# Causal latent attention and an eight-expert layer: projection and routing issued as single matmuls between the scores, own code for the first projection and the last routing, W1 loaded stack by stack

## The chip, the core and the metric

One core of a Trainium2 chip runs the whole program. The metric is the device time of one execution in microseconds (us); lower is better. The engines are PE (TensorE), DVE (VectorE), ACT (ScalarE), POOL (GpSimd) and SP (SyncE, which here only issues DMAs and waits). Each has its own in-order instruction stream; semaphores order them against each other.

## The reference

Four sequences of 1024 tokens, 256 channels, fp32. An attention block with 16 heads of 16 channels and a latent of 64 for keys and values, then a mixture of experts that sends each token to the two best of eight experts:

```python
xn   = layernorm(x)                                # x: (4, 1024, 256)
c_kv = xn @ W_DKV                                  # (.., 64)
k, v = c_kv @ W_UK, c_kv @ W_UV                    # 16 heads of 16
q    = xn @ W_UQ
ctx  = softmax(causal(q k^T / 4)) @ v
x    = x + ctx @ W_O
xf   = layernorm(x)
topw, topi = top_k(xf @ Wr / temp, 2); topw = softmax(topw)
for e in range(8):
    a, g = split(xf @ W1[e] + b1[e], 2)
    out += (a * silu(g) @ W2[e] + b2[e]) * weight_of(e)
x    = x + out
```

## The kernel before

**Two phases.** `fused_phase` does the attention, the output projection, the router, and scatters each token's normalised row into the lists of its two experts in DRAM (`slot_rows`). `expert_phase` then runs over 71 tiles of 128 rows of these lists. The change touches only the first phase.

**The step loop.** Every engine's stream in the fused phase is one Python loop over steps `s`. The work is cut into 16 quads (four heads of one sequence) of 12 units; a unit is one step. In step `s` PE computes the four score blocks whose row maxima DVE takes (`max_scores`, line 1009, line 1020 in the trace; DVE lines 745 and 748; three PSUM banks between them), the four score blocks of a unit `LEAD` = 16 steps earlier, with the maxima folded in as two extra rows (`prob_scores`, line 1039; ACT takes the exponential, line 961; three banks), and the product with V of a unit 18 steps earlier (`products`, line 1060, into one bank). POOL masks the diagonal blocks (`causal`, line 600). After the maxima of a quad are complete, PE turns them (line 1071), ACT copies them to SBUF (line 952), and SP writes them into the stack of Q by four DMAs (line 425). `TOTAL` is 192 steps; a sequence is a `PERIOD` of 48.

**Projection.** A chunk is 512 tokens, two to a sequence. SP loads x, DVE takes the statistics (`chunk_norm`), POOL the inverse root and the normalised rows (`normalise`, line 572), and PE then has nine steps, one group each (`project`, line 1074): two of four transposes (line 1081), the latent (line 1086), two for q (line 1093), two for k (line 1097), two for v (line 1101). A group is issued as a block at the end of the step, after `products`, into the one bank `x_aux_ps`; ACT copies it out at the start of the next step. POOL splits q and k into two float parts (`split`, lines 580 and 582), SP stores them, and later loads the stacks of a quad from there (`load_stack`, line 404). The loop starts at step -48, so the two chunks of the first sequence go through the same code with no scores beside them; chunks 2 to 7 run beside the scores from steps 6 and 17 of each period.

**Routing.** For each sequence: the softmax denominators are inverted and spread by DMA (lines 457 and 462), POOL scales the heads (line 610), four PE groups apply W_O (line 1111), ACT copies, POOL adds the residual (line 618), DVE takes statistics, POOL normalises (line 624), four PE groups transpose (line 1121), PE computes the logits (line 1131), DVE chooses the experts and the slots, POOL scatters 16 times (line 646). Sequences 0 to 2 are routed beside the scores of the next; for the last, the same code runs after the scores, one group after the other through `x_aux_ps`.

**Weights.** W1 lies where the stacks were and W2 where the probabilities were. ACT issues all 16 loads (12 MB) after the last product (`load_weights`, line 964).

## Time and profile before

| | us |
|---|---|
| median of 3 runs | 1404.23 |
| lowest and highest run | 1403.85, 1408.58 |
| the profiled execution | 1409.86 |
| its span | 1408.1 |
| PE busy | 1162.7 (83%) |
| DVE busy | 694.8 (49%) |
| ACT busy | 497.5 (35%) |
| POOL busy | 476.7 (34%) |

The profile is one execution. Times in its rows are us from the start of its span, means of one instruction are ns. "PEclk" is TensorE's granted clock as a share of full speed: 1.00 is 2.4 GHz, 0.50 is 1.2 GHz, and a value between is a stretch with both. A row of a timeline has start, duration, engine, line, instruction, tiles and count, and in brackets how long the engine was idle before it and what ended that. "PEld" is the loading of the stationary operand. A row of a window has the stretch and its length, the busy time and the number of instructions of PE, PEld, DVE, ACT and POOL, PEclk, the mean busy share of the 16 DMA engines, and GB/s moved. A busy PE is not a PE at its peak: matmuls are pipelined, and the durations overlap.

### The profile page before, as it was taken

To read this page: it belongs to the slowest core of one execution; us is meant where nothing else is said; L and a number is where in the kernel's file an instruction comes from. 1 tells how busy PE (TensorE), PEld (TensorE's weight loads), DVE (VectorE), ACT (ScalarE), POOL (GpSimd) and SP (SyncE) were. 2 spreads that over 40 slices of the span, in tenths; PEclk is the share of its full clock that TensorE was granted. 3 is DMA by queue.
4 is the path that set the end of the run, shared out by engine and by line. 5 is a ranking of instruction groups with operands and counts; after the bars stand their busy time and mean duration, and the time that the engine had idled before them with its cause. 6 is when DMAs were issued, how large, how long until landed. Compare 5 with 4: busy or idle time off the path is not lost. (4 is left out here: it accounts for less than half of the span.)

```text
span 1408.1 us, 19071 instructions
## 1 busy us (share of the span) xinstructions
PE 1162.7 (83%) x5236; PEld 612.5 (43%) x5237; DVE 694.8 (49%) x2121; ACT 497.5 (35%) x1077; POOL 476.7 (34%) x547
## 2 busy tenths in 40 slices
PE   3577999898989798989998870332999999999995
PEld 1234444344444334534445320221666666666663
DVE  1065587555665455576665400130555555555553
ACT  1102576554645454555554540010222222222221
POOL 6324313424425633424145330442222222222222
PEclk9655999879857697775588655555999999999998
DMA  2576343365404454322510129415222222222222
GB/s 81 173 129 174 100 96 70 113 177 138 100 8 136 143 165 111 69 57 83 153 55 17 40 76 346 112 61 194 39 46 47 46 45 45 45 45 45 45 45 34
DMA packets 94890, 130.39 MB, mean 93 GB/s; under 512 B 26208, under 2 KB 71136, under 8 KB 94816
## 3 DMA queue, kind: packets, MB, share of 16 engines
q1 hardware_dynamic: 64608, 89.51, 23.7%
q0 software_dynamic: 13296, 17.77, 7.7%
q10 hardware_dynamic: 16912, 22.23, 5.4%
q8 instruction: 34, 0.56, 0.2%
q14 instruction: 40, 0.33, 0.1%
HBM read 74.60 MB, written 54.22 MB: 91 GB/s over the span
## 5 line engine op out<-in xcount | busy, mean ns | idle before, releaser
L961 ACT ACTIVATE m_prob<-b_prob_ps 128x512 f32<-128x512 f32 (+3 forms) x768 | 326.2, 496 | 191.1 <-PE b_prob_ps L1039 185.8
L745 DVE CUSTOM_DVE_ANT_0 b_max_ps<-b_max_ps,b_mask_max 128x256 f32<-128x256 f32 (+3 forms) x512 | 245.9, 503 | 265.8 <-PE b_max_ps L1020 265.1
L1020 PE MATMUL b_max_ps<-m_stacks 48*128 48x512 f32 (+3 forms) x768 | 301.9, 501 | 54.9 <-DVE b_neg_max L745 29.5
L1039 PE MATMUL b_prob_ps<-m_stacks 50*128 50x512 f32 (+3 forms) x768 | 293.9, 483 | 27.6 <-DMA m_stacks<-b_max_rows 15.1
L1020 PEld LDWEIGHTS b_max_ps<-m_stacks 48*128 48x128 f32 x768 | 160.6, 237 | 234.1 <-DVE b_neg_max L745 111.3
L1268 POOL DMA_INDIRECT out_dram<-e_y,e_token x71 | 111.1, 1565 | 323.2 <-DVE e_y L1320 311.9
L1060 PE MATMUL b_acc_ps<-m_prob,b_v_aug 128*32 128x512 f32 (+3 forms) x1536 | 218.5, 651 | 0.2 <-POOL m_prob L600 0.2
L748 DVE TENSOR_REDUCE b_neg_max<-b_max_ps 128x1 f32<-128x512 f32 x256 | 176.1, 688 | 58.6 <-PE b_max_ps L1020 57.8
L600 POOL TENSOR_SCALAR_AFFINE_SELECT m_prob<-m_prob 128x512 f32<-128x512 f32 x128 | 80.6, 638 | 335.4 <-ACT m_prob L961 335.0
L1039 PEld LDWEIGHTS b_prob_ps<-m_stacks 50*128 50x128 f32 x768 | 150.7, 235 | 69.6 <-ACT m_prob L961 34.4
L1387 PE MATMUL e_g_ps<-m_w,e_rowsT 128*128 x284 | 135.5, 600 | 0.5 <-DVE e_rowsT L1288 0.5
L1404 PE MATMUL e_y_ps<-m_w,e_hiddenT 128*128 x568 | 134.4, 379 | 1.8 <-ACT e_hiddenT L1350 1.8
L1387 PE MATMUL e_a_ps<-m_w,e_rowsT 128*128 x284 | 133.9, 594 | 0.0
L1404 PEld LDWEIGHTS e_y_ps<-m_w,e_hiddenT 128*128 128x128 f32 x568 | 107.8, 190 | 46.2 <-issue 35.2
L1345 ACT ACTIVATE e_gate<-e_g_sum 128x512 f32<-128x512 f32 x71 | 44.7, 629 | 166.4 <-DVE e_g_sum L1300 166.4
L1350 ACT ACTIVATE e_hiddenT<-e_hiddenT_ps 128x512 f32<-128x512 f32 x71 | 42.4, 597 | 168.3 <-PE e_hiddenT_ps L1395 168.3
L1300 DVE TENSOR_TENSOR e_g_sum<-e_g_ps,e_b 128x512 f32<-128x512 f32 x71 | 49.1, 692 | 83.8 <-PE e_g_ps L1387 83.8
L1111 PE MATMUL x_aux_ps<-c_wo,c_heads 128*128 128x256 f32 x128 | 40.1, 467 | 55.7 <-POOL c_heads L610 53.6
L1387 PEld LDWEIGHTS e_a_ps<-m_w,e_rowsT 128*128 128x128 f32 x284 | 54.3, 191 | 68.8 <-issue 68.8
L1303 DVE TENSOR_TENSOR e_hidden<-e_a_ps,e_b 128x512 f32<-128x512 f32 x71 | 49.1, 691 | 71.0 <-PE e_a_ps L1387 71.0
L745 DVE DVE_READ_ACCUMULATOR2_ANT b_neg_max<- 128x1 f32 x512 | 72.3, 141 | 0.0
L1387 PEld LDWEIGHTS e_g_ps<-m_w,e_rowsT 128*128 128x128 f32 x284 | 48.9, 192 | 35.4 <-issue 35.4
(148 smaller groups left out, 1049.2 us busy)
## 6 DMA issues: line engine op xcount, KB each, us to landing
e_rows<-slot_rows ACTq DMA_DIRECT2D x73, 129.0 KB, 2.1
q_parts<-a_part SPq DMA_DIRECT2D x16, 512.0 KB, 2.7
k_parts<-a_part SPq DMA_DIRECT2D x16, 512.0 KB, 3.0
m_stacks<-q_parts SPq DMA_DIRECT2D x32, 256.0 KB, 5.2
m_stacks<-k_parts SPq DMA_DIRECT2D x32, 256.0 KB, 7.2
ctx_cols<-b_ctx_out SPq DMA_DIRECT2D x16, 512.0 KB
m_w<-in_L_ffn_W ACTq DMA_DIRECT2D x8, 1024.0 KB, 17.7
a_x<-in_L_attn_x SPq DMA_DIRECT2D x8, 512.0 KB, 4.1
```

The source lines that it names most:

```text
L600: nc.gpsimd.affine_select(out=tile, in_=tile, compare_op=ALU.is_ge, fill=0.0, base=0, pattern=[[0, QUAD], [1, P]], channel_multiplier=-1). ...
L745: nc.vector.tensor_tensor_reduce(scores, scores, mask_max[:, HALF - width:HALF], -1.0, -MASKED, ALU.add, ALU.min, to).then_inc(max_done, 1)
L748: nc.vector.tensor_reduce(to, scores, AX.X, ALU.max, negate=True).then_inc(max_done, 1)
L961: nc.scalar.activation(prob[:, n % NP, 0:width], prob_ps[n % NS][:, 0:width], ACT.Exp, scale=SCALE).then_inc(prob_ok, 1)
L1020: nc.tensor.matmul(out_ps[:, 0:width], q_st[g % RING][at:at + STACK, j, i * P:(i + 1) * P], k_st[g % RING][at:at + STACK, j, half * HALF:h ...
L1039: nc.tensor.matmul(prob_ps[n % NS][:, 0:width], k_st[g % RING][at:at + MAXROWS, pair, j * P:(j + 1) * P], q_st[g % RING][at:at + MAXROWS, ...
L1060: mm = nc.tensor.matmul(acc_ps[32 * h:32 * h + 2 * HD, first:first + width], v_aug[g % 2][:, j, h, :, :].rearrange("p r s -> p (r s)"), pr ...
L1268: nc.gpsimd.indirect_dma_start(out=out, out_offset=bass.IndirectOffsetOnAxis(ap=token[c % B][:], axis=0), in_=y[c % B][:], in_offset=None, ...
L1300: nc.vector.tensor_tensor(g_sum[c % 2][:], g_ps[c % 2][:], bias_of(expert, 0, FF, FF), ALU.add).then_inc(g_sum_ok, 1)
L1303: nc.vector.tensor_tensor(hidden[c % 2][:], a_ps[c % 2][:], bias_of(expert, 0, 0, FF), ALU.add).then_inc(a_sum_ok, 1)
L1387: last = nc.tensor.matmul(out_ps[:], rowsT[c % 2][:, d * P:(d + 1) * P], w1_sb[:, bass.ds(expert, 1), d, first:first + FF].rearrange("p e ...
L1404: last = nc.tensor.matmul(y_ps[c % 2][:], hiddenT[c % 2][:, f * P:(f + 1) * P], w2_sb[:, bass.ds(expert, 1), f, :].rearrange("p e n -> p ( ...
```

## The change

- **Projection beside the scores.** A chunk has 12 steps instead of nine: the latent and each q group are cut into their two matmul calls, one to a step. The PE work of a step (`aux`) comes after the second of the four score pairs, not at the end; ACT's copy comes after the third exponential of the same step. W_O is cut in the same way (8 steps instead of 4). The chunks start at steps 7 and 19.
- **DVE normalises** the chunk and the routed rows; POOL did both.
- **First projection.** Chunks 0 and 1 have code of their own ahead of the loop, which now starts at step 0. It uses all eight PSUM banks. ACT copies the high part straight from PSUM, DVE subtracts. Before the first score PE and DVE wait for the small weights, as before (`small_in`); SP now issues those behind the first stack, the last parts, V and the load of V.
- **Last routing.** The last sequence has code of its own behind the loop: heads scaled and residual added by DVE, four banks, transposed rows copied by ACT and DVE in turn.
- **Weights.** SP loads two experts' W1 whenever one of the last four stacks is no longer read; the last two and all of W2 are issued behind the last sequence's spread.
- **Order of SP's work.** A stack is loaded 12 steps ahead of its quad, was 18; x2 is loaded after the spread; some later steps of the routing are one to six steps later.

```diff
-CHUNK_AT = [6, 17]
-CHUNK_STEPS = 9
+CHUNK_AT = [7, 19]
+CHUNK_STEPS = 12
+GROUP_OF = [0, 1, 2, 2, 3, 3, 4, 4, 5, 6, 7, 8]
+SPLIT_AT = [6, 8, 9, 10]
-SPREAD_AT, ADD_AT, NORMAL_AT = 26, 28, 37
-ROUTER_AT, COUNT_AT, SCATTER_AT = 42, 46, 50
+HEADS_AT, ADD_AT, NORMAL_AT = 27, 32, 44
+ROUTER_AT, COUNT_AT, SCATTER_AT = 48, 52, 55
...
@@ sync @@
+            for n in range(4):
+                store_start_part(n)
+            load_stack(0)
+            for n in range(4, 8):
+                store_start_part(n)
+            for n in range(4):
+                store_start_v(n)
+            load_x(2)
+            load_v(0)
+            sp.dma_start(wo[:], w_o.rearrange("(c p) n -> p c n", p=P)).then_inc(small_in, 16)
+            sp.dma_start(wr[:], w_r.rearrange("(c p) n -> p c n", p=P)).then_inc(small_in, 16)
+            sp.dma_start(temp_in[:], temp.rearrange("(o n) -> o n", o=1).to_broadcast([P, 1])).then_inc(small_in, 16)
+            for s in range(LAST):
...
+                if u == 0 and NQUAD - RING <= g < NQUAD - 1:
+                    free_stack(g)
...
+            load_x2(LATE)
+            load_heads(LATE)
+            spread_den(LATE)
+            free_stack(NQUAD - 1)
+            sp.wait_ge(pv_ok, TOTAL)
+            for e in range(EXPERTS):
+                sp.dma_start(w2_sb[:, e, :, :], w2[e].rearrange("(f p) n -> p f n", p=P)).then_inc(w_in[e], 16)
...
@@ vector @@
+            def normalise(chunk, t):
+                if t == 0:
+                    dve.wait_ge(rstd_ok, chunk - 1)
+                    if chunk > 2:
+                        dve.wait_ge(aux_ps_ok, aux_at["project", chunk - 1, TURN_GROUPS - 1] + 1)
+                nc.vector.tensor_scalar(xn[:, t, :], x_in[:, t, :], mean_var[:, t, 0:1], rstd[:, t:t + 1],
+                                        ALU.subtract, ALU.mult).then_inc(xn_ok, 1)
...
+            def start_rest(n):
+                dve.wait_ge(start_hi_ok, n + 1)
+                nc.vector.tensor_tensor(start_part[n][:, 1, :].bitcast(F32R), start_ps[(6 + n) % 8][:],
+                                        start_part[n][:, 0, :], ALU.subtract).then_inc(start_lo_ok, 1)
...
+            invert(LATE)
+            for k in range(2 * DC):
+                late_heads(k)
+            for t in range(PAIRS):
+                late_residual(t)
+                late_statistics(t)
+            batch_norm(LATE)
+            for t in range(BT):
+                normalise2(LATE, t)
...
@@ scalar @@
+                for q in range(QUAD):
+                    if 0 <= s - LEAD < TOTAL:
+                        exponential((s - LEAD) * QUAD + q)
+                    if q == 2:
+                        aux_copies(s)
...
@@ tensor @@
+            start_turn(0)
+            start_turn(1)
+            pe.wait_ge(w_project_in, 32)
+            start_latent(0)
+            start_latent(1)
...
+            for n in range(4):
+                start_values(n)
+            pe.wait_ge(start_lo_ok, 8)
+            pe.wait_ge(start_v_ok, 4)
+            pe.wait_ge(const_ok, ROUTE_CONSTS)
+            pe.wait_ge(small_in, 48)
+            for s in range(LAST):
...
+                for q in range(QUAD):
+                    n = s * QUAD + q
+                    if s < TOTAL:
+                        max_scores(n)
+                    if 0 <= s - LEAD < TOTAL:
+                        prob_scores(n - LEAD * QUAD)
+                    if q == 1:
+                        aux(s)
+                if 0 <= s - LEAD - LAG < TOTAL:
+                    products(s - LEAD - LAG)
+            for t in range(PAIRS):
+                late_add(t)
+            for t in range(PAIRS):
+                late_normal(t)
```

## Rows read from the trace of the kernel before

**Rows 1.** Windows: the four stages of the run.

```profile
0.00:74.49 74.49, 31.93 (x65) 12.53 (x66) 4.36 (x22) 12.04 (x20) 35.80 (x62) 0.80 0.44 128
74.49:838.24 763.75, 690.50 (x3526) 321.97 (x3526) 442.94 (x1535) 389.62 (x902) 289.39 (x371) 0.74 0.38 99
838.24:974.65 136.41, 23.13 (x82) 17.84 (x83) 17.82 (x66) 8.76 (x13) 40.41 (x44) 0.53 0.54 166
974.65:1408.00 433.35, 417.17 (x1564) 260.14 (x1564) 229.72 (x498) 87.08 (x142) 111.08 (x71) 0.98 0.29 52
```

**Rows 2.** Timeline of the first stage, rows of POOL, PE and SP.

```profile
11.22 4.85 POOL L572 TENSOR_SCALAR a_xn<-a_x,a_mv,a_rstd 128x256 f32<-128x256 f32 x4
...
19.79 3.67 PE L1086 MATMUL x_aux_ps<-a_xnT,a_wdkv 128*64 128x512 f32 x4 [0.69 <-ACT a_xnT L900]
...
24.14 1.98 PE L1093 MATMUL x_aux_ps<-a_xnT,a_wuq_rh 128*128 128x512 f32 x4 [0.68 <-ACT a_ckvT L902]
...
29.49 1.12 PE L1097 MATMUL x_aux_ps<-a_ckvT,a_wuk_rh 64*128 64x512 f32 x2 [0.69 <-ACT a_raw L909]
...
62.97 1.73 SPq L404 DMA_DIRECT2D m_stacks<-q_parts  x4
...
74.49 0.87 PE L1020 MATMUL b_max_ps<-m_stacks 48*128 48x256 f32 x3 [13.13 <-DMA m_stacks<-k_parts]
```

**Rows 3.** Windows: the end of the first stage, with the DMA rate.

```profile
35.00:70.00 35.00, 18.86 (x39) 7.54 (x37) 0.00 (x0) 6.56 (x11) 14.26 (x15) 0.65 0.56 175
```

**Rows 4.** Waits of SP: us in total, times, longest us.

```profile
SPq L437 <- DMA ctx_cols<-b_ctx_out: 23.1, 4, 9.0
...
SPq L462 <- DMA inv_dens<-c_inv_den: 15.6, 4, 12.0
```

**Rows 5.** Timeline of the last routing, all engines.

```profile
867.92 1.33 SPq L462 DMA_DIRECT2D c_spread<-inv_dens  x2
...
889.18 4.92 POOL L610 TENSOR_TENSOR c_heads<-c_heads,c_spread 128x512 f32<-128x512 f32 x4 [49.30 <-DMA c_spread<-inv_dens]
...
891.81 3.75 PE L1111 MATMUL x_aux_ps<-c_wo,c_heads 128*128 128x256 f32 x8 [53.63 <-POOL c_heads L610]
...
908.99 0.25 POOL L554 TENSOR_SCALAR c_var_eps<-c_mv 128x8 f32<-128x8 f32 x1 [1.62 <-DVE c_mv L782]
...
912.25 9.67 POOL L624 TENSOR_SCALAR c_first_row<-c_x,c_mv,c_rstd 128x256 f32<-128x256 f32 x8
```

**Rows 6.** Timeline of SP: the spread of the first sequence.

```profile
318.01 1.37 SPq L462 DMA_DIRECT2D c_spread<-inv_dens  x2
```

**Rows 7.** Timeline of POOL: the first user of that spread.

```profile
328.52 1.28 POOL L610 TENSOR_TENSOR c_heads<-c_heads,c_spread 128x512 f32<-128x512 f32 x1 [3.13 <-DMA c_spread<-inv_dens]
```

**Rows 8.** Timeline of ACT: copies of the turned maxima, twelve steps apart.

```profile
167.11 0.27 ACT L952 ACTIVATE b_max_rows<-b_max_ps 64x128 f32<-64x128 f32 x1 [1.59 <-PE b_max_ps L1071]
...
197.85 0.27 ACT L952 ACTIVATE b_max_rows<-b_max_ps 64x128 f32<-64x128 f32 x1 [0.53 <-PE b_max_ps L1071]
...
658.46 0.27 ACT L952 ACTIVATE b_max_rows<-b_max_ps 64x128 f32<-64x128 f32 x1 [1.78 <-PE b_max_ps L1071]
...
701.51 0.27 ACT L952 ACTIVATE b_max_rows<-b_max_ps 64x128 f32<-64x128 f32 x1 [1.78 <-PE b_max_ps L1071]
```

**Rows 9.** Windows: two stretches of the score stage at 1.2 GHz.

```profile
269.00:300.00 31.00, 29.84 (x124) 13.87 (x117) 12.57 (x36) 12.16 (x32) 14.09 (x17) 0.50 0.61 158
631.00:716.00 85.00, 84.16 (x370) 36.62 (x368) 48.27 (x156) 41.11 (x95) 26.35 (x33) 0.50 0.39 105
```

**Rows 10.** Timeline of ACT where it waits for POOL.

```profile
267.33 0.60 ACT L909 ACTIVATE a_raw<-x_aux_ps 128x512 f32<-128x512 f32 x1 [3.14 <-POOL a_part L582]
```

**Rows 11.** Windows of tile x_aux_ps on PE: length, PE busy (instructions), clock, DMA.

```profile
143.00:838.00 695.00, 121.50 (x397) 0.76 0.35 94
```

**Rows 12.** Timeline of a step at 2.4 GHz, one row of PE.

```profile
201.86 0.50 PE L1020 MATMUL b_max_ps<-m_stacks 48*128 48x512 f32 x1 [0.50 <-DVE b_neg_max L745]
```

**Rows 13.** The instructions of line 1320: duration ns min/median/max.

```profile
L1320 DVE TENSOR_SCALAR e_y<-e_y,e_rows x71: 352/353/451, 994.2 to 1396.4; 128x256 f32<-128x256 f32 x71
```

More of the change, by code:

```diff
@@ L244, in fused_phase @@
         second_row = sb("c_second_row", [P, BT, ROW])
+        start_x, start_xn, start_xnT, start_ckvT = x2, first_row, heads, spread[0:LAT, 0, :]
+        start_part = [prob[:, START_PARTS + 2 * n:START_PARTS + 2 * n + 2, :] for n in range(6)] + [
+            part[n][:].bitcast(F32) for n in range(2)]
         tokens = [P, BT, EXPERTS]
```

657 lines of the change are left out of this document (429 added, 228 removed).

## Prediction, made before the changed kernel ran

> **What bounds the kernel now.** I read the windows by stage first, then a timeline of each stage, then the waits. Four stages follow each other with almost no overlap [rows 1]: projection of the first sequence, 74.5 us; the scores, 763.8 us; the last routing, 136.4 us; the experts, 433.4 us. The last isn't touched, so the sum is made over the first three. In the first and the third PE is busy 32 and 23 us: these are chains, not loads. In the second PE is busy nine tenths of the time at a mean clock of 0.74. As the clock has only the levels 2.4 and 1.2 GHz (1.00 and 0.50), that is about 48% of the stage, 367 us, at the upper one and 397 us at the lower.
>
> What the lower level costs is seen where little else than scores runs: twelve steps take 197.85 - 167.11 = 30.7 us early on and 701.51 - 658.46 = 43.1 us late [rows 8], the latter inside a stretch at 0.50 throughout [rows 9]. So a us at 2.4 GHz becomes 1.40 at 1.2, and one at 1.2 gives back 0.29.
>
> **First stage.** Chunk 0's chain starts as before. From the normalised rows on (11.2 us), two chunks now go through it: eight rows of 0.35 on DVE, taken from a DVE instruction of the same shape [rows 13], against 4.85 for four on POOL [rows 2]; some 4.4 of transposes; two latents of 3.67; four q groups of 1.98; four k groups of 1.12 [rows 2]. 11.2 + 2.8 + 4.4 + 7.3 + 7.9 + 4.5 = 38.1, plus one copy after the transposes and one after the latent, 39. The first stack needs only the first four parts, which are out some 6 us earlier, at 33 to 34, and landed by 38. Before, stack loads issued from 62.97 gave the first score at 74.49, 11.5 us later [rows 2]. By that alone the scores would start at 49.5.
>
> Something else is late then. PE and DVE wait for the three small loads (`small_in`) before the first score, and SP now issues them last: behind the stack (1.5 MB), four parts (2 MB), V (1 MB) and the wait for V to land. 4.5 MB from 38 on at the 175 GB/s of the last such stretch [rows 3] end at 64; at one and a half times that rate (the stretch had its DMA busy 0.56 of the time) at 55. Then come the issue and the landing of the small loads, some 4 us, estimated from the like steps. I take 60, between 50 (if they come in time) and 68. **Gain 14, from 6 to 24.** Behind PE's wait stands the whole score stage, behind DVE's the maxima.
>
> **Last routing.** From the last copy of the context to the scaled heads it takes 50 us now. Three pieces of that lie beside 12 MB of weights on ACT's queue. The store of the context was waited for 9.0 us, the other three times (23.1 - 9.0)/3 = 4.7; the inverse denominators 12.0 against (15.6 - 12.0)/3 = 1.2 [rows 4]; the spread took 889.18 - 867.92 = 21.3 [rows 5] against 328.52 - 318.01 = 10.5 for the first sequence [rows 6, 7], itself beside other stores. The change puts six experts' W1 before the end and the rest behind the spread. Gain 4.3 + 10.8 + 10.8 = 26; less (13) if the x2 load ahead or the weights right behind still crowd these transfers, up to 31 if the spread beats its row. Moved W1 loads, three times 2 MB on SP's queue, stand ahead of the stores and of `load_max_rows` of the last quads; twelve steps last 30 us or more, 2 MB some 8, so I cost them at nothing; with that cover gone, 1 to 2 us of PE each.
>
> The Trainium skill (DMA: Bandwidth & Descriptors, the paragraph "Arbitration") says that a DMA engine takes turns between the queues that have work, packet by packet. By that rule two queues halve the spread's rate and one queue in order doesn't, which is the 21.3 against 10.5 above; the sum would stay.
>
> From the first scaled head to the router: heads by DVE, 1.2 earlier; the four W_O groups in four banks without copies between, 17.2 us between 891.81 and 908.99 [rows 5], of which 4 x 3.75 at half clock can't go, gain 2; the eight normalised rows 2.8 instead of 9.67 [rows 5, 13], gain 6.9. **Together 26 + 10 = 36, from 23 to 44.** What follows (logits, choice, sixteen scatters, the first rows of the experts) is the same work. W2 is in long before its first use: 6 MB behind the spread is some 20 us, and more than 60 us of chain follow.
>
> **Scores.** Projection and routing hold PE 121.5 us between 143 and 838 [rows 11], with the sixth chunk, before that stretch, some 136. The matmuls are the same ones. At the end of a step they are paid in full: DVE and ACT run dry behind them. Between two score pairs they can hide in what PE waits for anyway: in a clean step at 2.4 GHz PE stands 0.50 us for a bank that DVE holds [rows 12], and one matmul call is 1.98/2 = 0.99. So half of it hides, and only at the upper clock; at 1.2 GHz PE had no such gap (84.2 of 85 us busy, [rows 9]). The mean of 0.76 there [rows 11] is 0.52 of the time at the upper level: 136 x 0.52 x 0.5 = 35. Bounds: 0 and 70.
>
> DVE gains 24 normalised rows of the chunks and 24 of the routes, 48 x 0.353 = 17 us [rows 13]. At 2.4 GHz it is nearly as loaded as PE, so 0.52 of that is paid: -9 (0 to -17). The rows go off POOL, and with them a collision: at 267.3 ACT had waited 3.14 us for POOL's split [rows 10], exponentials stood behind that copy and PE behind them, and then the clock was low for 31 us [rows 9]. This falls once in each later pair of chunks, twice. 2 x (3.1 + 31 x 0.29) = 24; I take 20, since the clock may fall for another reason a little later. **Sum 35 - 9 + 20 = 46, from -17 to 94.** Stacks loaded 12 steps ahead instead of 18 cost nothing: 11.5 us [rows 2] against 30.7; were that cover gone, each of 15 quads would wait.
>
> **Total.** 14 + 36 + 46 = 96. The profiled execution took 1409.9 (span 1408.1), so 1314; it lies 5.7 above the median of the three runs. Median 1404.2 - 96 = **1308**.
>
> **Rivals.**
> - *The clock stays up.* One matmul in nearly every step, and fewer stalls, hold the upper level through most of the scores. All 397 us at 1.2 GHz would give back 397 x 0.29 = 115; half to three quarters of that, less the 20 already counted, is 37 to 66: 1308 becomes some 1255. The Trainium skill (TensorE: Matmul & The Clock Gate, "Part 1: The HAM clock gate") has activity release the clock and idleness lower it, which speaks for this. Against it stands a row: from 631 to 716 PE was busy 84.2 of 85 us and the clock remained 0.50 [rows 9].
> - *The scores give nothing.* Inserted between pairs, the calls cost what they cost at the end, and DVE's new work is paid. Only the ends gain: 1404 - 50 = 1354, between 1340 and 1375. For it: half the stage has a saturated PE.
> - *Slower.* Spread thin, projection and routing no longer lift the clock. The stretch at 0.50 ended at 716 beside such work, and what was dense is now one call to a step. If all 367 us at 2.4 GHz went to 1.2: 367 x 0.40 = 147, and 1404 - 50 + 147 = 1501. It decides from 50/0.40 = 125 us of lost upper clock on. Against it: early in the stage pure scores held 1.00 for a whole quad (30.7 us for twelve steps).
> - *The change doesn't do what it says*: the small loads hold the start at 74, and another transfer holds the spread; with scores unchanged, about 1400.
>
> **How the numbers follow.** Forecast 0.50 (1280 to 1335), clock up 0.20, scores give nothing 0.23, slower 0.05, no effect 0.02. The range leaves out the lower third of the clock case (0.07), the upper part of the third (0.05) and the last two (0.07): 1245 to 1362. About 0.5%, 7 us, is what a measurement here can tell from no change. Faster 0.93, same 0.02, slower 0.05.
>
> **What would show it.** The first score near 60, with PE's wait ended by a small load or DMA, not by the stack. From the last context copy to the first scaled head 20 to 28 us, not 50; the logits some 36 us sooner after that copy than now. In the score stage a mean clock of 0.70 to 0.85 and twelve clean steps still near 31 us at 1.00; ACT no longer waiting for `split`. DVE's normalising rows near 0.35. I am wrong if the score stage is not shorter by 20 to 80 us, above all if its clock has left that band, or if a transfer at either end waits on something that I put at nothing.

## The result, and the profile after

| | before | after |
|---|---|---|
| median of four runs, us | 1406.4 | 1377.9 |
| lowest and highest | 1403.85, 1427.19 | 1361.48, 1398.81 |
| the profiled execution | 1409.86 | 1362.01 |

The changed kernel is faster: ratio 0.9688, 95% interval 0.9645 to 0.9732, some 44 us (0.0312 x 1404.2). The forecast was 96. Executions of one and the same kernel differ here in the clock that TensorE was granted, so the ratio goes by the undisturbed ones (after: 1361.48 and 1362.01 us at a mean clock of 0.795 and 0.796; it leaves out 1393.85 and 1398.81 at 0.771 and 0.764), while the medians below are those of all executions and a few numbers are given at equal clock.

The windows by stage of the changed kernel, with the columns of [rows 1]:

```profile
0.00:60.06 60.06, 23.03 (x65) 11.71 (x66) 16.28 (x41) 10.24 (x17) 11.49 (x38) 0.87 0.56 165
60.06:824.43 764.37, 686.03 (x3526) 300.29 (x3526) 476.96 (x1584) 393.41 (x902) 226.54 (x318) 0.72 0.40 106
824.43:926.76 102.33, 20.14 (x82) 17.83 (x83) 27.12 (x84) 5.17 (x7) 25.53 (x33) 0.55 0.56 167
926.76:1359.90 433.14, 417.38 (x1564) 260.72 (x1564) 229.80 (x498) 87.07 (x142) 110.67 (x71) 0.98 0.29 52
```

Against [rows 1]: the first stage 60.06 us instead of 74.49 (14.4 less), the scores 764.37 instead of 763.75 (nothing), the last routing 102.3 instead of 136.4 (34.1 less), the experts alike. Start and last routing came as forecast; all that is missing is missing from the scores.

**Start.** Timeline, the first score, and SP's issues of the stack and of the small loads:

```profile
36.59 1.73 SPq L465 DMA_DIRECT2D m_stacks<-q_parts  x4
...
54.84 0.36 SPq L478 DMA_DIRECT2D b_v_in<-v_rows  x1
55.24 0.58 SPq L562 DMA_DIRECT2D c_wo<-in_L_attn_W_O  x1
55.87 0.47 SPq L563 DMA_DIRECT2D c_wr<-in_L_ffn_Wr  x1
56.38 0.47 SPq L564 DMA_DIRECT2D c_temp<-in_L_ffn_temp  x1
...
60.06 0.87 PE L1243 MATMUL b_max_ps<-m_stacks 48*128 48x256 f32 x3 [19.50 <-DMA c_temp<-in_L_ffn_temp]
```

PE stood 19.5 us, and what ended it was a scalar, `c_temp`, not the stack issued at 36.59. SP reached the small loads only at 55.24, behind V.

**Last routing.** Timeline of all engines, the rows that answer to [rows 5]:

```profile
824.43 0.60 ACT L1133 ACTIVATE b_ctx_out<-b_acc_ps 128x512 f32<-128x512 f32 x1 [2.89 <-PE b_acc_ps L1283]
...
838.80 0.33 SPq L515 DMA_DIRECT2D inv_dens<-c_inv_den  x1
840.72 1.33 SPq L520 DMA_DIRECT2D c_spread<-inv_dens  x2
...
854.14 2.50 DVE L907 TENSOR_TENSOR c_heads<-c_heads,c_spread 128x512 f32<-128x512 f32 x4 [15.37 <-DMA c_spread<-inv_dens]
...
875.47 6.97 PE L1353 MATMUL x_aux_ps<-c_wr,c_heads 128*128 128x8 f32 x32 [0.83 <-issue]
```

The first scaled head comes 29.7 us after the context copy (854.14 - 824.43), before 50.9. The spread took 13.4 us, before 21.3 [rows 5].

**Scores.** PE was idle for 78.3 us of the stage (764.37 - 686.03), before 73.3 [rows 1], though the waits that the prediction spoke of are smaller. The list of PE's waits (total, times, longest) names a new one at its head:

```profile
PE b_prob_ps L1262 <- DMA m_stacks<-b_max_rows: 44.3, 6, 18.5
...
PE b_max_ps L1243 <- DVE b_neg_max L827: 22.9, 35, 4.1
```

These are the rows of maxima, 8 KB a load, that SP writes into the stack (`load_max_rows`) one step before the first probability scores of a quad read them. Before, this wait was 15.1 us, 4.6 at most. Of the 44.3 us, 39.4 fall into three holes, one in each sequence that is routed beside scores. Timeline around the first of them, SP and PE and POOL:

```profile
289.42 1.37 SPq L520 DMA_DIRECT2D c_spread<-inv_dens  x2
290.75 0.27 ACT L1141 ACTIVATE b_max_rows<-b_max_ps 64x128 f32<-64x128 f32 x1 [0.46 <-PE b_max_ps L1294]
290.83 0.46 SPq L527 DMA_DIRECT2D c_x<-in_L_attn_x  x1
292.56 2.12 SPq L441 DMA_DIRECT2D q_parts<-a_part  x1
294.72 3.46 SPq L488 DMA_DIRECT2D m_stacks<-b_max_rows  x4
...
302.27 1.26 POOL L696 TENSOR_TENSOR c_heads<-c_heads,c_spread 128x512 f32<-128x512 f32 x1 [3.52 <-DMA c_spread<-inv_dens]
...
306.04 0.61 POOL L666 CAST a_part<-a_raw 128x512 fp32r<-128x512 f32 x1 [1.93 <-DMA q_parts<-a_part]
...
306.82 0.79 PE L1262 MATMUL b_prob_ps<-m_stacks 50*128 50x512 f32 x1 [9.92 <-DMA m_stacks<-b_max_rows]
...
509.19 0.79 PE L1262 MATMUL b_prob_ps<-m_stacks 50*128 50x512 f32 x1 [10.95 <-DMA m_stacks<-b_max_rows]
...
688.89 0.79 PE L1262 MATMUL b_prob_ps<-m_stacks 50*128 50x512 f32 x1 [18.50 <-DMA m_stacks<-b_max_rows]
```

ACT has the rows at 291.0. SP issues them at 294.72, behind the spread (1 MB), x2 (1 MB, which the change moved from the load of the heads to here) and a part (0.5 MB). They land when these 2.5 MB are through: the spread is used at 302.27, the room that the part's store frees at 306.04, the rows at 306.82. The stack (1.5 MB), issued three steps ahead of the rows instead of nine, stands in front as well. The Trainium skill (DMA: Bandwidth & Descriptors, "Arbitration") has the engines take turns between queues; within one queue these rows show none of that, 8 KB waited for 2.5 MB.

The longest hole has a second piece. SP and ACT around the third:

```profile
657.48 2.72 SPq L465 DMA_DIRECT2D m_stacks<-k_parts  x4
...
662.71 0.34 SPq L515 DMA_DIRECT2D inv_dens<-c_inv_den  x1
664.85 0.27 ACT L1141 ACTIVATE b_max_rows<-b_max_ps 64x128 f32<-64x128 f32 x1 [0.53 <-PE b_max_ps L1294]
672.21 1.33 SPq L520 DMA_DIRECT2D c_spread<-inv_dens  x2
...
674.10 4.94 SPq L488 DMA_DIRECT2D m_stacks<-b_max_rows  x4
```

Here ACT had the rows at 665.1, but SP issued them only at 674.10: it stood up to 9.1 us until the store of the inverse denominators, issued right behind the stack, had landed. From SP's list of waits (total, times, longest):

```profile
SPq L520 <- DMA inv_dens<-c_inv_den: 13.9, 4, 9.1
```

So two small transfers wait in that queue, and the second holds SP itself.

### The profile page after: what moved, and what is told of

It is laid out like the page before. It is cut to its first block and busy times, and to the rows that moved or that the text cites. A ratio compares the mean times of both kernels' runs of the same rounds, so it can differ in the third digit from the quotient of the medians.

```text
span 1359.9 us, 19012 instructions
## 1 busy us (share of the span) xinstructions
PE 1146.6 (84%) x5236; PEld 590.6 (43%) x5237; DVE 750.2 (55%) x2206; ACT 495.9 (36%) x1068; POOL 374.2 (28%) x459
## 5 line engine op out<-in xcount | busy, mean ns | idle before, releaser
L1149 ACT ACTIVATE m_prob<-b_prob_ps 128x512 f32<-128x512 f32 (+3 forms) x768 | 340.8, 495 | 306.4 <-PE b_prob_ps L1262 300.7
L1262 PE MATMUL b_prob_ps<-m_stacks 50*128 50x512 f32 (+3 forms) x768 | 305.8, 493 | 49.3 <-DMA m_stacks<-b_max_rows 44.3
L1243 PE MATMUL b_max_ps<-m_stacks 48*128 48x512 f32 (+3 forms) x768 | 300.7, 493 | 45.5 <-DVE b_neg_max L827 22.9
L1243 PEld LDWEIGHTS b_max_ps<-m_stacks 48*128 48x128 f32 x768 | 151.8, 234 | 264.3 <-DVE b_neg_max L827 126.4
L1283 PE MATMUL b_acc_ps<-m_prob,b_v_aug 128*32 128x512 f32 (+3 forms) x1536 | 209.7, 628 | 1.3 <-POOL m_prob L686 1.3
L1713 PEld LDWEIGHTS e_y_ps<-m_w,e_hiddenT 128*128 128x128 f32 x568 | 108.0, 190 | 46.0 <-issue 35.2
L1683 PE MATMUL e_rowsT_ps<-e_ident,e_rows 128*128 128x128 f32 x144 | 28.1, 278 | 41.3 <-DMA e_rows<-slot_rows 41.3
```

The lines of the kernel that those rows point to most:

```text
L1149: nc.scalar.activation(prob[:, n % NP, 0:width], prob_ps[n % NS][:, 0:width], ACT.Exp, scale=SCALE).then_inc(prob_ok, 1)
L1243: nc.tensor.matmul(out_ps[:, 0:width], q_st[g % RING][at:at + STACK, j, i * P:(i + 1) * P], k_st[g % RING][at:at + STACK, j, half * HALF:h ...
L1262: nc.tensor.matmul(prob_ps[n % NS][:, 0:width], k_st[g % RING][at:at + MAXROWS, pair, j * P:(j + 1) * P], q_st[g % RING][at:at + MAXROWS, ...
L1283: mm = nc.tensor.matmul(acc_ps[32 * h:32 * h + 2 * HD, first:first + width], v_aug[g % 2][:, j, h, :, :].rearrange("p r s -> p (r s)"), pr ...
L1713: last = nc.tensor.matmul(y_ps[c % 2][:], hiddenT[c % 2][:, f * P:(f + 1) * P], w2_sb[:, bass.ds(expert, 1), f, :].rearrange("p e n -> p ( ...
```

## The experiments

The ratios are to the kernel before, timed beside each version; none is on record for e1 and e5. Since the clock differs between executions, the last columns put every run at a mean clock of 0.80 with the slope that the runs of one kernel show among themselves (130 runs, 10.0 us for each 0.01 of clock). In e13 one execution at a clock of 0.607 (1617 us) is left out of these columns. That column is a way to read the runs and no cause: what a kernel does may set its clock too.

| run | what | median us | ratio (interval) | clock | at 0.80 |
|---|---|---|---|---|---|
| | before | 1411.8 | | 0.797 | 1412 |
| | after | 1377.9 | 0.969 (0.965-0.973) | 0.782 | 1361 |
| e1 | x2 as before | 1375.7 | | 0.783 | 1352 |
| e2 | spread behind rows | 1336.2 | 0.940 (0.927-0.954) | 0.803 | 1337 |
| e3 | stack earlier | 1368.7 | 0.966 (0.955-0.978) | 0.789 | 1356 |
| e4 | e2 and e3 | 1327.3 | 0.939 (0.930-0.948) | 0.810 | 1337 |
| e5 | two queues | 1358.7 | | 0.792 | 1349 |
| e6 | e4, end of step | 1365.8 | 0.971 (0.963-0.979) | 0.798 | 1365 |
| e7 | e4, POOL normalises | 1336.8 | 0.952 (0.944-0.960) | 0.801 | 1338 |
| e8 | e4, small loads early | 1325.7 | 0.941 (0.932-0.950) | 0.801 | 1327 |
| e10 | e4, late weights | 1345.0 | 0.943 (0.933-0.953) | 0.807 | 1350 |
| e11 | e8 and x, x2 early | 1307.3 | 0.917 (0.907-0.926) | 0.810 | 1319 |
| e13 | e4, dense | 1323.3 | 0.938 (0.926-0.950) | 0.820 | 1339 |
| e14 | e6, dense | 1363.0 | 0.965 (0.958-0.972) | 0.796 | 1359 |
| e17 | e11, dense | 1342.0 | 0.953 (0.945-0.962) | 0.787 | 1330 |
| e12 | before, rows first | 1391.9 | 0.984 (0.981-0.988) | 0.811 | 1403 |
| e9 | before, inserted | 1445.9 | 1.020 (1.011-1.030) | 0.778 | 1420 |
| e15 | e9, rows first | 1441.4 | 1.026 (1.015-1.036) | 0.771 | 1411 |
| e16 | e15, DVE normalises | 1413.6 | 1.003 (0.996-1.009) | 0.788 | 1401 |

### Is it the one queue? (e1 to e5)

The theory: the rows of maxima wait in SP's queue behind large transfers. Rivals: SP only issues them late; what PE no longer waits for them it waits for DVE. The first edit is e1, the second e2, the third e3; e4 is the second and the third.

```diff
 if at_route(s, HEADS_AT - 6):
     load_heads(at_route(s, HEADS_AT - 6)[0])
+    load_x2(at_route(s, HEADS_AT - 6)[0])
 if at_route(s, HEADS_AT - 2):
     spread_den(at_route(s, HEADS_AT - 2)[0])
-    load_x2(at_route(s, HEADS_AT - 2)[0])
```

> The changed kernel with one load put back: x2 (1 MB) goes with the load of the heads, four steps ahead of the spread, as before the change, and no longer right behind the spread. Theory (one queue in order): PE's 44.3 us of waiting for the rows of maxima come from tiny transfers (8 KB) that stand in SP's queue behind the spread, x2, a part and the stack. In the changed trace 2.5 MB issued from 289.42 were through at 306, so 1 MB is some 6.6 us; three sequences, so the waits for the rows fall from 44 to some 27 us and the ratio to the kernel before from 0.969 to 0.957. Rival (the issue is late, not the transfer): SP is held by its own waits, and x2 out of the way changes nothing, 0.969. Rival (the backlog only moves): x2 with the heads pushes the stack back by the same 1 MB, and the waits keep over 38 us, 0.965 to 0.969.

Measured: the waits for the rows fell from 44.3 to 28.5 us (longest 9.7), as expected to 2 us. So bytes in front of them are what they wait for, and the backlog doesn't simply move. The median stayed at 1375.7, at the changed kernel's mean clock (0.783 and 0.782); at 0.80, where every execution is put at the same clock, it is 9 us faster, of an expected 17.

```diff
 for s in range(LAST):
+    if turned_at(s - 1) is not None:
+        load_max_rows(turned_at(s - 1))
...
-                if at_route(s, HEADS_AT - 2):
-                    spread_den(at_route(s, HEADS_AT - 2)[0])
-                    load_x2(at_route(s, HEADS_AT - 2)[0])
+                if at_route(s, HEADS_AT - 5):
+                    store_inverse(at_route(s, HEADS_AT - 5)[0])
+                if at_route(s, HEADS_AT - 3):
+                    spread_den(at_route(s, HEADS_AT - 3)[0])
+                    load_x2(at_route(s, HEADS_AT - 3)[0])
```

`HEADS_AT` is 30 here, so the inverse denominators are stored in step 25 of the sequence as before and the spread goes in step 27. `store_inverse` is the first half of `spread_den`.

> The changed kernel with the rows of maxima first in each step of SP, and the spread and x2 behind them (three steps later than now, POOL's scaling three steps later too); the stacks as in the changed kernel. Theory (one queue in order): only the tail of the stack stands ahead of the rows, so the three long waits (9.9, 11.0 and 18.5 us) fall to 3 us or less each, the sum from 44 to some 12: ratio 0.946 by that alone. The clock fell at 300, 502 and 672, in these waits, and stayed low for 41, 34 and 34 us; if they caused that, up to 109 x 0.29 = 31 us more come back, 0.924. Rival (the clock falls for another reason): it falls a little later all the same, the mean clock of the score stage stays 0.72, 0.946. Rival (insertion costs what the end of the step cost): what PE no longer waits for the rows it waits for DVE, under 15 us come back, 0.96.

Measured: no wait for the rows is left in the list, and 1336.2 us, 0.940. PE now waits 18.8 us, four times, for POOL's masking (`b_acc_ps <- POOL m_prob`; 1.3 us in the changed kernel). The expected 0.946 was for the rows alone, 0.924 with the clock; the mean clock of the score stage was 0.72, that of the changed kernel. The rival on the clock holds: the falls at 300, 502 and 672 were not what kept it low. The rival on DVE is out, its wait is 25.3 us against 22.9. The rival that SP only issues the rows late isn't told apart here, since they now go ahead of SP's wait as well; e1 is against it for the first two holes (9.9 and 11.0 us became 5.2 and 8.6, with the rows still issued behind the spread), e3 for the third.

```diff
-g, u = divmod(s + UNITS, UNITS)
-if u == 0 and 0 < g < NQUAD:
+g = stack_at(s)
+if g is not None:
     load_stack(g)
```

> The changed kernel with the stacks loaded 18 steps ahead as before the change (the first of a sequence 9 ahead, behind the rows of maxima, since its parts are not stored sooner), not 12 ahead, which is three steps in front of the rows. The prediction put this move at nothing. Theory (one queue in order): 1.5 MB leave the queue ahead of the rows; the wait at 248.86 (3.3 us) goes and the three long ones lose some 2 to 5 us each, together 8 to 15: ratio 0.958 to 0.963. Rival (the move costs nothing, as predicted): spread and x2 alone make the waits, under 3 us, 0.967 to 0.970.

> Both moves of SP's work together: rows of maxima first, spread and x2 behind them, stacks 18 steps ahead. Theory (one queue in order): nothing large is left ahead of the rows, their waits fall from 44 to under 6 us: ratio 0.942 from that alone, 0.92 if the upper clock comes back as well (mean of the score stage 0.78 and more). Rival (the clock falls for another reason): 0.942, mean clock 0.72. Rival (insertion hides nothing): waits for DVE take the place of those for the rows, 0.955 or more.

e3: waits for the rows 35.2 instead of 44.3 us, 0.966; 9 us of waiting as expected, but the time can't be told from the changed kernel's (at equal clock 5 us less). Eight of the nine are in the third hole, 10.5 instead of 18.5 us: with the stack out of the way SP's longest wait for the inverse denominators is 1.2 us, not 9.1. Putting that move at nothing was wrong, by about what a measurement shows. e4: no wait for the rows, 0.939, hardly more than e2. The windows of its score stage:

```profile
60.66:796.18 735.52, 678.19 (x3526) 292.34 (x3526) 474.52 (x1584) 393.72 (x902) 226.56 (x318) 0.73 0.43 110
```

28.8 us shorter than in the changed kernel, of which 21 are idle time (57.3 against 78.3). Not all 44 us came back: in e4 POOL waits 9.5 us, until 506.91, for a part's store that now stands behind spread and x2, causal masks stand behind POOL, and PE waits 8.55 us for them. It is the same in the first sequence, so the first two holes only changed their owner: 9.9 and 11.0 us behind the rows became 9.0 and 8.6 behind POOL's masks. Most of the idle time that came back is the third hole, 18.5 us, where 4.0 are left (for scaled heads). The queue is as full as ever; the order only picks who waits. PE in e4:

```profile
313.71 1.51 PE L1297 MATMUL b_acc_ps<-m_prob,b_v_aug 128*32 128x384 f32 x8 [9.00 <-POOL m_prob L700]
...
509.51 1.51 PE L1297 MATMUL b_acc_ps<-m_prob,b_v_aug 128*32 128x384 f32 x8 [8.55 <-POOL m_prob L700]
...
679.54 2.04 PE L1346 MATMUL x_aux_ps<-c_wo,c_heads 128*128 128x256 f32 x4 [3.96 <-POOL c_heads L710]
```

For e5 these loads go to ACT's stream:

```diff
+                if at_route(s, HEADS_AT - 1):
+                    spread_den(at_route(s, HEADS_AT - 1)[0])
+                    load_x2(at_route(s, HEADS_AT - 1)[0])
                 if at_route(s, COUNT_AT):
                     power_of(at_route(s, COUNT_AT)[0])
```

> The changed kernel, in which ACT issues the spread and x2 of the first three sequences on its own queue, one step later than SP does now; SP's order is otherwise that of the changed kernel (rows of maxima behind a part and the stack). Theory (the rows wait in SP's queue behind the large transfers): in a queue of their own the large transfers no longer stand ahead of them, though the bytes are the same and move at the same time; PE's waits for the rows fall from 44 to under 15 us, ratio to the kernel before 0.945 to 0.95. Rival (the DMA engines as a whole are busy, whichever queue): the waits stay over 30 us, 0.96 to 0.97.

Measured: waits for the rows 15.0 us, so the queue matters and not only the DMA engines as a whole. In the first two sequences spread and x2 were still issued before the rows (302.43 and 304.65 us, 503.24 and 503.90), one step later than in the changed kernel, and PE waited 6.9 and 3.5 us instead of 9.9 and 11.0; in the third the rows went first (668.19, the spread 674.51), and no wait is left. The time is 1358.7, less gain than expected, with a wait that I had not foreseen. ACT must wait for the inverse denominators to land before it may issue the spread, and in the third sequence, behind the stack again, they were slow:

```profile
665.75 0.34 SPq L515 DMA_DIRECT2D inv_dens<-c_inv_den  x1
...
674.51 1.22 ACTq L1170 DMA_DIRECT2D c_spread<-inv_dens  x2
675.83 0.41 ACTq L1177 DMA_DIRECT2D c_x<-in_L_attn_x  x1
676.34 1.22 ACT L1152 ACTIVATE m_prob<-b_prob_ps 128x256 f32<-128x256 f32 x4 [8.18 <-issue]
```

ACT's exponentials stood 8.2 us behind that wait and PE 7.15 behind them. The queue that is free of large transfers belongs to an engine on the path.

### What the place of the matmuls is worth (e6, e13, e14)

```diff
-        if q == 1:
-            aux(s)
     if 0 <= s - LEAD - LAG < TOTAL:
         products(s - LEAD - LAG)
+    aux(s)
```

> The version with both moves of SP's work (0.939), and in it the matmuls of projection and routing at the end of each step behind the products, as before the change, with ACT's copies at the start of the next step; one call to a step as in the changed kernel. Theory of the prediction (between two score pairs half of each call hides at 2.4 GHz): 136 us x 0.46 of the time at the upper level x 0.5 = 31 us are paid again, ratio 0.961, and DVE waits for PE behind the calls. Rival (insertion hides nothing, PE is saturated): 0.939 within 0.006. Rival (it is the spreading over more steps that hides them, not the place in the step): 0.939 to 0.945.

Measured: 1365.8 against 1327.3, 38 us (28 at equal clock); expected 31. The size fits, the mechanism only in part: PE waits 74 times for a bank that DVE holds instead of 35 times (37.0 and 23.4 us), but of the 30 us by which the profiled score stage is longer only 7 are idle time of PE (64.3 against 57.3); the other 23 are in its busy time, and why isn't shown. Two windows of score stages, e6 and then e13 (between the pairs, whole groups):

```profile
60.28:825.96 765.68, 701.37 (x3526) 322.44 (x3526) 467.67 (x1584) 388.93 (x903) 226.52 (x318) 0.73 0.41 106
```

```profile
60.95:775.29 714.34, 652.09 (x3526) 288.68 (x3526) 476.10 (x1584) 392.40 (x902) 227.84 (x318) 0.77 0.44 113
```

e13 and e14 differ from e4 and e6 by the groups of a chunk's projection (W_O stays cut), and its splits come two to three steps sooner:

```diff
-CHUNK_STEPS = 12
-GROUP_OF = [0, 1, 2, 2, 3, 3, 4, 4, 5, 6, 7, 8]
+CHUNK_STEPS = 9
+GROUP_OF = [0, 1, 2, 3, 4, 5, 6, 7, 8]
...
-SPLIT_AT = [6, 8, 9, 10]
+SPLIT_AT = [4, 5, 6, 7]
```

> The version with both moves of SP's work (0.939), in which a chunk's projection takes nine steps again, one whole group to a step (both matmuls of a latent or q group in one place), still between the second and third score pair; routing as it is. The kernel before with its groups moved between the pairs was 2% slower, while the same version with its single matmuls put at the end of the step was 38 us slower: place and spreading do not add up. Theory (the copy that each group waits for, one step earlier, is late for dense groups, and PE then waits between the pairs, where nothing covers it): the score stage goes from 736 to 750 or more, ratio 0.950 to 0.965. Rival (in the kernel before it was POOL's normalising and SP's order that made the place bad): no change here, 0.939.

> The version with single matmuls at the end of the step (score stage 765.7), in which a chunk's projection takes nine steps, whole groups, as before the change. The kernel before with the rows of maxima first had a stage of 747.0 in this form. Theory (spreading over more steps costs by itself, since each step with a call ends in a stall of DVE and ACT; the prediction had put it at nothing): 750 to 758, ratio 0.958, so spreading cost some 12 and the place gave 38 only against that. Rival (spreading is free, the rest of the difference is DVE's normalising and the clock): 765, 0.966.

The square, medians in us: between the pairs 1327 (single) and 1323 (whole groups), at the end 1366 and 1363; at equal clock 1337 and 1339, 1365 and 1359. The place is worth 38 to 40 by the medians and 28 and 20 at equal clock; whether the rest, which is clock, comes from the place isn't shown. Cutting the projection's groups into single matmuls brought nothing that can be measured. My theory for both runs, that spreading had a price or a use of its own, is out.

### The normalising (e7)

```diff
-                nc.vector.tensor_scalar(xn[:, t, :], x_in[:, t, :], mean_var[:, t, 0:1], rstd[:, t:t + 1],
+                nc.gpsimd.tensor_scalar(xn[:, t, :], x_in[:, t, :], mean_var[:, t, 0:1], rstd[:, t:t + 1],
```

and in `normalise2` likewise.

> The version with both moves of SP's work (0.939), and in it the normalising of the chunks and of the first three routed sequences on POOL, as before the change (48 instructions of 1.2 us there against 0.35 on DVE). Theory of the prediction: DVE gives back 9 us, the collisions with the splits and the causal masks on POOL cost 20, so 11 us slower, ratio 0.947. Rival (the collisions need not come back, since the splits now stand apart): DVE's 9 us are the larger term, 0.933. Rival (neither is on the path): 0.939.

Measured: 9.5 us slower than e4, near the expected 11; but at equal clock it is 1 us, the intervals overlap, and the profiled score stages are 736.5 and 735.5. So no price of either is shown. The collision is another matter. In the kernel before ACT waited 14.7 us, four times, for POOL's split; that wait is gone from the changed kernel's list, as forecast, but it is gone from e7's too, where POOL normalises, and it is there with 15.4 us in e16 below, where DVE does. So it went with something else in the changed schedule, and not with the rows' move to DVE. The first rival had that much right.

### The start and the last routing (e8, e10, e11)

```diff
+            sp.dma_start(wo[:], w_o.rearrange("(c p) n -> p c n", p=P)).then_inc(small_in, 16)
+            sp.dma_start(wr[:], w_r.rearrange("(c p) n -> p c n", p=P)).then_inc(small_in, 16)
+            sp.dma_start(temp_in[:], temp.rearrange("(o n) -> o n", o=1).to_broadcast([P, 1])).then_inc(small_in, 16)
             for n in range(4):
                 store_start_part(n)
             load_stack(0)
```

> The version with both moves of SP's work (0.939) and two more: the three small loads stand ahead of the stores of the first parts on SP, and the spread and x2 of the first three sequences go on ACT's queue. Theory for the start (the 60 us are the small loads, as predicted): the first score comes at 49 to 51 us instead of 60, PE's wait ended by the stack, 10 us less. Theory for the queue: a wait of 8.6 us of PE at 509, for POOL, which waited 9.5 us for a part's store behind the spread and x2 in SP's queue, goes as well. Ratio 0.939 - 18/1410 = 0.926. Rival for the start (V or the masks from POOL come later than 50): 57 or more, 0.935. Rival for the queue (the store is slow with two queues too): the 8.6 us stay, 0.932.

Timeline, PE and then DVE:

```profile
48.19 0.87 PE L1273 MATMUL b_max_ps<-m_stacks 48*128 48x256 f32 x3 [6.81 <-DMA m_stacks<-k_parts]
...
57.03 1.41 DVE L853 BATCH_NORM_STATS2 a_stats<-a_x 128x6 f32<-128x256 f32 x4 [6.23 <-DMA a_x<-in_L_attn_x]
...
59.28 1.30 PE L1273 MATMUL b_max_ps<-m_stacks 48*128 48x384 f32 x2 [7.86 <-DVE b_neg_max L838]
```

The first score comes at 48.19, ended by the stack: the 49.5 "by the stack alone" of the prediction were right. But 7.9 of the 12 us go at once, because DVE's statistics of the third chunk, in step 0, wait for an x that SP loads behind V. PE's wait behind POOL went from 8.6 to 4.8 us and not to nothing, so a part of it stays with two queues too, as the rival for the queue had it. So 0.941, where 0.926 was expected (at equal clock 10 us better than e4).

```diff
+            load_x(2)
             for n in range(4):
                 store_start_part(n)
...
-                if at_route(s, HEADS_AT - 3):
-                    load_x2(at_route(s, HEADS_AT - 3)[0])
+                if at_route(s, HEADS_AT - 15):
+                    load_x2(at_route(s, HEADS_AT - 15)[0])
```

> The version with both moves of SP's work (0.939), with the small loads and the x of the third chunk ahead of the stores of the first parts, the spread on ACT's queue, and x2 there 12 steps sooner than the spread. In the run with the small loads early the first score came at 48.19, but DVE waited 6.2 us for that x behind V, and PE 7.9 us for DVE. Theory: this wait goes, POOL's wait for a part's store (6.3 us) as well, the score stage keeps its 736 us or less and the 12 us of the start stay: ratio 0.939 - 16/1410 = 0.928, some 1308 us. Rival (the score stage hands back what starts earlier, through the clock): the stage is over 744 us, 0.935 to 0.94.

With that x in front too, and x2 12 steps sooner, the stage begins at 47.76 and takes 729.3 us: 1307.3 us, 0.917, the fastest version. Here the gain of the start stays (at equal clock 18 us better than e4).

The weights of e10, in ACT's stream behind the loop, as the kernel before has them; SP's loads are gone:

```diff
+            act.wait_ge(pv_ok, TOTAL)
+            for e in range(EXPERTS):
+                act.dma_start(w1_sb[:, e, :, :], w1[e].rearrange("(c p) n -> p c n", p=P)).then_inc(w_in[e], 16)
+                act.dma_start(w2_sb[:, e, :, :], w2[e].rearrange("(f p) n -> p f n", p=P)).then_inc(w_in[e], 16)
             late_turned(0)
```

> The version with both moves of SP's work (0.939), in which the expert weights go as before the change: all 12 MB on ACT's queue behind the last copy of the context, beside SP's transfers of the last routing. Theory of the prediction (of the 34 us that the last routing gained, the larger part is that these transfers no longer share the DMA engines with the weights): the time from the last context copy to the first scaled head goes from some 30 back to some 45 us, ratio 0.950. Rival (the gain is from x2 loaded first and the heads scaled by DVE): 30 to 33 us, 0.940. The score stage gains what the W1 loads cost there, if anything.

```profile
816.38 0.32 SPq L523 DMA_DIRECT2D inv_dens<-c_inv_den  x1
822.05 1.33 SPq L531 DMA_DIRECT2D c_spread<-inv_dens  x2
842.32 1.29 DVE L914 TENSOR_TENSOR c_heads<-c_heads,c_spread 128x512 f32<-128x512 f32 x2 [25.96 <-DMA c_spread<-inv_dens]
```

The spread takes 20.3 us again (842.32 - 822.05), the first scaled head comes 49.6 us after the context copy (at 792.76), 19 to 20 later than in the changed kernel; the whole routing is 121.7 us against 101.2 in e4. So the weights beside it were 20 of the 34 us.

e17 is e11 with the groups of e13.

> The fastest version so far (0.9165: rows of maxima first, stacks earlier, small loads and third x first, spread on ACT's queue with x2 12 steps sooner), with the chunks' projection in nine steps as whole groups. Between the pairs dense was no slower than spread (1323 against 1327 us). Theory (spreading gives nothing, dense frees the steps before the heads): 1290 to 1305 us, 0.915. Rival (dense parts leave POOL and SP's queue as the spread comes, and collide with x2): 1315 or more, 0.93.

This missed: 1342.0, slower than e11, with the rows of maxima waited for again (20.7 us, six times, 4.8 at most) and a mean clock of 0.69 in the score stage. The rival (a collision in SP's queue) has the wait on its side, but the larger part of the loss is the clock (at 0.80: 1330 against 1319).

### The same parts in the kernel before (e9, e12, e15, e16)

e12 and e15 have the two lines of e2 that put `load_max_rows` first in SP's step, e9, e15 and e16 this one for PE (and ACT's copies behind its third exponential):

```diff
+                    if n % QUAD == 1:
+                        aux(s)
                 if 0 <= s - LEAD - LAG < TOTAL:
                     products(s - LEAD - LAG)
-                if at_chunk(s, 0, CHUNK_STEPS):
-                    project(*at_chunk(s, 0, CHUNK_STEPS))
```

> The kernel before, in which SP issues the rows of maxima ahead of everything else of a step. PE waited for them 15.1 us in it (five times, 4.6 at most), behind part and V stores and a spread three steps ahead. Theory (one queue in order, and the waits are paid in full): 8 to 12 us less, ratio 0.992 to 0.994, within what can be told from no change. Rival (the waits are hidden in others): 1.0. Either is small; what it tells apart is whether the changed kernel's loss was already there (then over 20 us, 0.985) or came with the change.

Measured 0.984, 20 us: more than the wait itself, which went from 15.1 to 8.9. PE's clock in the score stage rose from 0.74 to 0.77. At equal clock 9 us. So a part of what e2 and e4 win back was lost in the kernel before already.

> The kernel before, with one thing of the change alone: projection and routing are called between the second and the third score pair of a step, whole groups in as many steps as before, and ACT copies between its exponentials; start, last routing, POOL's normalising and SP's order stay. Putting the calls back to the end of the step in the changed kernel had cost 38 us. Theory (the place in the step hides them): some 30 us less here, ratio 0.978, between 0.973 and 0.985. Rival (only single matmuls spread over more steps fit between the pairs; a group of 1.98 us stalls DVE and ACT as much as at the end): 0.993 to 1.0. Rival (POOL's normalising and the collisions are what is late then): 0.99.

Slower by 2% (8 us at equal clock), against both rivals too. PE's waits, e9:

```profile
PE x_aux_ps L1115 <- POOL c_heads L610: 57.5, 5, 51.1
...
PE b_prob_ps L1043 <- DMA m_stacks<-b_max_rows: 28.2, 7, 6.2
PE x_aux_ps L1125 <- POOL c_first_row L624: 26.0, 13, 9.5
...
PE x_aux_ps L1105 <- ACT a_raw L909: 10.9, 5, 3.1
```

In the kernel before these four were 53.6 (1), 15.1 (5), 15.8 (7) and 3.5 (3). The calls come half a step sooner and what they need doesn't, so PE's in-order stream waits between two score pairs.

> The kernel before with its projection and routing called between the second and third score pair (1.020 by itself) and with the rows of maxima first in SP's steps (0.984 by itself). In the run with the place alone PE waited in the score stage for the rows 28.2 us (15.1 before), for POOL's normalised rows of the route 10 more than before, for POOL's scaled heads 6, for raw copies 7: together the 38 us by which the stage grew. Theory (the place is good, but PE's stream is in order and what the calls need comes late): the rows' part goes, 20 to 28 us, ratio 1.000 to 1.005. Rival (the place costs in the kernel before whatever SP does): only the 16 us of the rows-first run, 1.008. Rival (SP's order was all of it): 0.96.

> The same with the normalising of the chunks and of the route on DVE as well. Theory (POOL's late rows were the second part of what the place costs there): another 15 to 25 us, since DVE makes a row in 0.35 us against 1.2 and POOL's splits and masks come sooner: ratio 0.985 to 0.99, and the place is worth its 38 us only together with both. Rival (DVE's 17 us of new work are paid): no better than the run without it.

Both missed. e15: the wait for the rows fell to 12.5 us, the time hardly (1441.4; at equal clock 9 us less). e16: DVE's rows brought 28 us (11 at equal clock), and PE's wait for them fell to 13.8, but at 1.003 it is still behind e12, which has the calls at the end; at equal clock the two are level (1401 and 1403). The place pays 38 us in the changed schedule (20 to 28 at equal clock) and at best nothing in the old one. What of the new schedule it needs stays open. It isn't more room between scaling the heads and W_O: the changed kernel has five steps there, but e4 and e6, between which the 38 us were measured, have two (`HEADS_AT` 30, `ADD_AT` 32), as the kernel before has (26 and 28). Left untested are W_O in eight steps instead of four and the later steps of the routing.

## Why the prediction was wrong

The step that failed is the order of SP's work in the score stage: a stack that comes later was put at nothing, x2 behind the spread had no term. PE's wait for the rows of maxima grew from 15.1 to 44.3 us. The prediction's own sign of being wrong, a score stage not shorter by 20 to 80 us, came true: 764.4 against 763.8.

- **Start: right.** 14.4 us against 14, first score 60.06 against 60, and the wait ended by a small load. e8 and e11 show the other bound too.
- **Last routing: right.** 34.1 us against 36. The transfers gave 21.2 (50.9 - 29.7) where I had 26, since the spread took 13.4 us, not the 10.5 of an earlier one. The chain behind gave 12.9 against 10 (34.1 - 21.2).
- **Calls between the pairs: right in size.** 35 forecast, 38 measured (e4 against e6), 28 at equal clock. That half of each call hides in a gap of PE isn't shown: most of the difference is in PE's busy time.
- **Normalising: not for its reason.** Net 11 forecast, 9.5 measured, 1 at equal clock; the nearness is luck. The 20 us for the collision rested on POOL's rows being its cause, and in e7 it is still gone with them back on POOL. DVE's price was sized too low: a row took 0.53 us in the chunks and 0.41 in the route (medians), not 0.353: 48 of them are 22 us of DVE, not 17.
- **SP's queue: the step that failed.** "Stacks loaded 12 steps ahead instead of 18 cost nothing" asked only whether the stack itself is in time (it is) and not whom it stands in front of. And x2, which the diff moves right behind the spread, had no term in the sum at all. I had read the spread's own duration with care and never asked for the next small transfer behind it. The rows of maxima are issued one to two steps before their use; 2.5 MB and more in front of them cost 10 to 18.5 us a sequence. In the third sequence half of that is SP, held by a store behind the stack. Against e2 and e4 the ratios put it at 40 to 42 us, give or take 10 and more, and equal clock at 24. The list of waits of before had the line, 15.1 us, and it wasn't in my rows; by e12 some 9 of the 24 us were lost there already, so the change itself added some 15, an estimate.
- **Clock: a further part.** Over the whole span the executions that the ratio goes by had the clock of before (0.795 and 0.796 against 0.797), but the score stage had 0.72 against 0.74: inside the band of 0.70 to 0.85, at its low end. At 10.0 us for each 0.01 over a span of 1400 us, 0.02 over 764 us is some 11 us, an estimate.

For the score stage alone: place 28 and normalising 1 gained, queue 15 to 24 and clock 11 lost, which is the nothing that was measured. The sum at equal clock: start 14 + routing 34 + place 28 + normalising 1 - queue 24 = 53, measured 51 (1412 - 1361); with the 15 us that the change itself added to the queue it is 62, so some 11 us are not accounted for. With the queue mended (e4) the gain in medians is 88 us of the forecast 96, at equal clock 75. By the ratio the time is 0.9688 x 1404.2 = 1360, so the rival "the scores give nothing" (1354, up to 1375) had the time, but not for its reason: the calls did hide; a new wait and the clock took it back. The range ended at 1362: 16 us short of the median of the four runs and at the two that the ratio goes by, because no case in it had a new wait in the score stage.

What stays open: what sets the clock. In the score stage it was 0.77 in e12 and e13 and 0.69 in e17 and e15, for the same matmuls. Removing the holes didn't raise it (e2: 0.72). Open as well: what took the collision with the splits away, and what the place between the pairs needs.

## What to carry to other kernels

A transfer that is moved has two prices: whether it lands in time, and what stands behind it in its queue. Look for the smallest transfer with the shortest time between issue and use, and ask after every move what is now in front of it; put it first in its queue, then look who stands behind the large ones now (POOL's masks in e4), or issue the large ones well ahead of their use (x2 12 steps sooner in e11, the fastest version). A wait that goes away with a change may have gone for another reason: put the part of the change that was to remove it back, and see whether it returns (e7). A gain at the start or in an in-order stream is kept only if the next thing in line comes sooner as well: the DVE statistics behind x in e8, the scaled heads in e9.

## What the runs showed of the hardware that I had not expected

Within one queue an 8 KB load waited until 2.5 MB ahead of it were through, up to 10.5 us from issue to landing against a median of 1.9; the same bytes on a second queue, one step later, brought PE's waits from 44.3 to 15.0 us. And the same program differs by 10 us for each 0.01 of mean granted clock, from 1397 to 1444 us for the kernel before over 47 runs, so that two versions whose waits differ by 10 us can't be told apart without their clocks.
